# One core, a time-mix layer and then a routed block: statistics ahead of selection, another order on the scalar engine, and later gathers

## The chip, the cores and the metric

One core of a Trainium2 chip. The metric is device time in microseconds (us), from launch to end. A sequence's channels lie on the 128 partitions. The kernel is written for the engines directly, each with its own program and waits on semaphores: TensorE (PE), VectorE (DVE), ScalarE (ACT), GpSimd (POOL) and SyncE (SP, which issues loads and stores).

## What is computed

Two post-norm layers. The first, on 32 sequences of 512 tokens and 256 channels:

```python
x = layernorm(x + (sigmoid(r) * wkv(decay, first, k, v)) @ Wo)   # k, v, r from x mixed with its shift
# wkv: a = a*ew + exp(k)*v ; b = b*ew + exp(k), token by token
```

The second scores every token with a router (`x @ router_w`), takes per sequence the 63 best of 512, and runs a block on these alone:

```python
topv, topi = top_k(weights, 64); sel = sort(topi[:, :63])
x_sel, m_sel = x[sel], mask[sel][:, sel]
x1 = x_sel + softmax(rope(q) @ rope(k).T / 4 + m_sel) @ v @ wo   # 16 heads of 16
x2 = x1 + gelu(rmsnorm(x1) @ w1) @ w2
out = layernorm(x + scatter(x2 * weight) + x * (not selected))
```

## The kernel before

**First part (to 490 us).** A loop of 32 periods, one sequence each, written as four by hand, twelve in a loop over rings of four, and sixteen by hand. In period s the engines do:
- SP: `load_channels(s+2)`, `store_rows(s-3)`.
- POOL (`period`, L669): `differences_of(s+1)` (L561), `gate_of(s-1)` (L583), `mixes_of(s+1)` (three additions L567, one subtraction L568), `log_sum_of(s)` (L574), `scale_of(s-2)` (L590, L591). Every one is a tensor_tensor between buffers in SBUF but the copy L591.
- PE (L806): `projections(s)`, whose K, V and R parts each wait until DVE has done with the bank of sequence s-1 (`den_done`, `num_done`, `clamp_done`); `outputs(s-1)`; `selection(s)`.
- ACT (L1236): the exponentials, logarithms and reciprocals, `differences_scaled(s+1)` (L1185, L1186), `evacuation_of(s-1)` (L1193), `rows_of(s-3)` (L1215, the normalisation).
- DVE (L1561): `den_scan_of` (L1503), `den_of` (L1517), `products_of`, `clamp_of` (L1525), `num_of` (scans L1530, L1535), then `selection(s)`, then `statistics_of(s-1)` (L1544 to L1559).

The scans multiply by `ewb`, a [128, 2, 512] tile that the start fills with ones (L1455) and with the decay (L1483). Sequence 0 is mixed by DVE at the start (L1449, L1452); from sequence 1 on POOL and ACT mix.

**Selection.** The sequences fall into groups of 16, 12 and 4 (`SEQS`). For a group: `token_weights` (L1581 to L1587), PE turns them to rows, eight `top_round`s on DVE (a MAX8 L1624 and a MATCH_REPLACE8 L1626, the last without the replace), `slots_chosen` part 0 (L1635 to L1640) and part 1 (L1642 to L1644), PE turns the slots, `one_hot` (L1662) per pair, PE `picks`, `keep_values` (L1676 to L1686), which gives the row numbers for the gathers. Group 0's runs in periods 18 to 29; group 1's begins in period 29 and goes on in the attention.

**Attention (490 to 700 us).** Sixteen pairs of sequences. `att_period(n)` exists on each engine, and pairs overlap. PE's order (L1048) is: `mask_turn(n+1)` (L892), `project_qk(n)` (L917), `p_turn(n-2)` (L931), `project_v(n)`, `o_turn(n-3)` (L941), `scores(n-1)` (L967), `hn_turn(n+1)`, `mask_pick(n+1)` (L904), `values(n-2)`, `hn2_turn(n-4)`, `qk_turn(n)` (L975), `project_o(n-3)` with the group's turns and picks. ACT's order (L1351): `mask_copy`, `norm2_of(n-4)`, `pT_copy(n-2)`, `v_copy(n)`, in n = 1 the last sequences' variances, rows and roots, then `oT_copy`, `hnT_copy(n+1)` (L1233), `mask_keep`, `h2T_copy`, `exp_p(n-1)`, `q_copy`, `k_copy`. DVE's (L1855): `rope(n)`, `selection_early(n)`, `softmax_in(n-1)` (L1742 to L1746), `output_of`, `residual`, `selection_late(n)`. POOL's (L710): `normed2`, `rope_end`, gathers, `normed(n+2)`, `x_of(n+2)`, mask gathers. `x1`, the block's residual, lies from column 4096 of the arena, over the statistics' tiles.

**Last part (700 us to the end).** The feed-forward network over eight groups of two pairs, and the scatter. The change doesn't touch it.

## Time and profile before

| | us |
|---|---|
| median of 3 runs | 811.86 |
| lowest, highest | 810.51, 814.69 |
| the profiled execution | 812.5 |
| its span, first to last instruction | 810.8 |
| mean granted TensorE clock | 0.977 of 2.4 GHz |
| busy: PE, DVE, ACT, POOL | 92%, 83%, 65%, 61% |

A row of a timeline is: start, duration, engine, line, operation, output<-input, shape, count, and in brackets how long the engine was idle before it and what released it. "issue" as releaser means that no other engine's event shows. Rows of several instructions in a run are merged (x3), with the duration from the first's start to the last's end.

### The profile page before, as it was taken

Reading aid. Unit: us, or ns where it says so; the run is one execution under the profiler, and the core shown is the slowest. Engines: PE = TensorE matmul, PEld = TensorE weight load, DVE = VectorE, ACT = ScalarE, POOL = GpSimd, SP = SyncE. Lnnn points to the kernel's source line nnn. Section 1 sums busy time; section 2 is a strip of 40 time slices with the busy share of each in tenths; the row PEclk is TensorE's granted clock in tenths of the full one; section 3 lists DMA queues with packets and bytes.
Section 4 is the critical chain, followed back from the end, with each engine's and each line's share of the span. In section 5 each row is a group of like instructions: output and inputs, shape, how many; then the busy total and the mean of one; then the engine's idle time right before and its main releaser. Section 6 shows DMA issues by size and latency. Waiting matters only on the chain.

```text
span 810.8 us, 13316 instructions
## 1 busy us (share of the span) xinstructions
PE 743.9 (92%) x4482; PEld 551.1 (68%) x4482; DVE 675.3 (83%) x1382; ACT 523.7 (65%) x1015; POOL 498.5 (61%) x463
## 2 busy tenths in 40 slices
PE   7899999999999999899899986879998798899993
PEld 4566666666667666565557755667776577799993
DVE  7889989898989999999999999687798566257784
ACT  3668888888888887877666766646576566321120
POOL 1778878787878776787666995364556623202222
PEclk9999999999999999999999999899999899989998
DMA  8024232424232332332242112401110110000000
GB/s 227 2 65 118 80 116 65 129 65 125 69 107 88 96 100 66 101 94 65 68 120 73 46 50 88 143 27 47 39 36 14 50 43 2 1 1 28 27 20 34
DMA packets 37338, 55.41 MB, mean 68 GB/s; under 512 B 3360, under 2 KB 26528, under 8 KB 37280
## 3 DMA queue, kind: packets, MB, share of 16 engines
q1 hardware_dynamic: 34464, 46.28, 19.0%
q0 software_dynamic: 2816, 8.39, 3.4%
q8 instruction: 33, 0.54, 0.3%
q14 instruction: 25, 0.20, 0.1%
HBM read 35.78 MB, written 18.87 MB: 67 GB/s over the span
## 4 chain that ended last, share of the span: by engine, by line
PE 51%; DVE 24%; POOL 9%; issue 6%; ACT 6%; DMA 2%; SPq 0%; another core or an unknown queue 0%; POOLq 0%; DVEq 0%; ACTq 0%
PE ps L782 12%; PE ps L787 8%; PE ps L802 6%; PE ps L1112 5%; PE ps L1124 4%; POOL arena L567 4%; DVE arena L1503 3%; PE ps L917 2%; POOL arena L583 2%; PE ps L984 2%; DVE arena L1555 2%; PE ps L800 2%; DVE arena L1535 2%; DVE arena L1525 1%; DVE arena L1544 1%
## 5 line engine op out<-in xcount | busy, mean ns | idle before, releaser
L787 PE MATMUL ps<-halves 128*128 128x512 f32 x558 | 235.4, 530 | 0.0
L782 PE MATMUL ps<-arena,wa 128*128 128x512 f32 x384 | 201.9, 608 | 12.5 <-DVE arena L1535 4.4
L787 PEld LDWEIGHTS ps<-halves 128*128 128x128 f32 x558 | 106.0, 190 | 98.2 <-issue 89.9
L802 PE MATMUL ps<-wa,arena 128*128 128x256 f32 x512 | 133.0, 383 | 0.0
L583 POOL TENSOR_TENSOR arena<-arena 128x1024 f32<-128x1024 f32 x32 | 76.3, 2385 | 74.9 <-issue 53.1
L567 POOL TENSOR_TENSOR arena<-arena 128x512 f32<-128x512 f32 x93 | 116.8, 1288 | 5.3 <-ACT halves L1186 5.3
L782 PEld LDWEIGHTS ps<-arena,wa 128*128 128x128 f32 x384 | 69.8, 190 | 42.1 <-POOL halves L568 13.8
L802 PEld LDWEIGHTS ps<-wa,arena 128*128 128x128 f32 x512 | 88.2, 192 | 6.8
L1503 DVE TENSOR_TENSOR_SCAN arena<-ewb,ps 128x511 f32<-128x511 f32 x64 | 74.5, 1206 | 20.6 <-ACT ps L1158 19.2
L574 POOL TENSOR_TENSOR arena<-arena 128x1024 f32<-128x1024 f32 x32 | 76.4, 2387 | 23.6 <-ACT arena L1172 23.6
L1530 DVE TENSOR_TENSOR_SCAN arena<-ewb,ps 128x511 f32<-128x511 f32 x64 | 74.1, 1200 | 0.0
L1215 ACT ACTIVATE arena<-arena 128x256 f32<-128x256 f32 x128 | 66.1, 589 | 0.0
L638 POOL TENSOR_SCALAR arena<-arena,norm 128x256 f32<-128x256 f32 x16 | 16.6, 1036 | 74.5 <-ACT norm L1315 74.5
L1185 ACT ACTIVATE arena<-arena,cols 128x512 f32<-128x512 f32 x93 | 60.0, 710 | 0.0
L1344 ACT ACTIVATE arena<-ps 128x512 f32<-128x512 f32 x32 | 18.8, 598 | 61.6 <-PE ps L1112 61.6
L800 PE MATMUL ps<-ident,arena 128*128 128x128 f32 x256 | 49.5, 275 | 4.4 <-DVE arena L1555 2.8
L1112 PE MATMUL ps<-halves 128*128 128x256 f32 x384 | 50.4, 293 | 2.6 <-ACT arena L1336 2.6
L1112 PEld LDWEIGHTS ps<-halves 128*128 128x128 f32 x384 | 49.3, 202 | 3.2 <-ACT arena L1336 3.1
L1156 ACT ACTIVATE arena<-ps 128x1024 f32<-128x1024 f32 x32 | 32.6, 1020 | 26.2 <-PE ps L787 21.6
L800 PEld LDWEIGHTS ps<-ident,arena 128*128 128x128 f32 x256 | 35.9, 142 | 19.3 <-issue 3.8
L561 POOL TENSOR_TENSOR arena<-arena 128x512 f32<-128x512 f32 x31 | 41.5, 1339 | 12.1 <-DMA arena<-x_chan 12.0
L1124 PE MATMUL ps<-halves 128*128 128x256 f32 x384 | 47.5, 283 | 1.5 <-DVE halves L1893 1.5
(226 smaller groups left out, 1584.7 us busy)
## 6 DMA issues: line engine op xcount, KB each, us to landing
arena<-x_chan SPq DMA_DIRECT2D x32, 512.0 KB, 4.3
out<-arena SPq DMA_DIRECT2D x32, 512.0 KB, 3.3
arena<-x_chan SPq DMA_DIRECT2D x64, 127.8 KB, 3.4
wa<-w_attn SPq DMA_DIRECT2D x1, 1024.0 KB, 7.1
wa<-w_up SPq DMA_DIRECT2D x1, 1024.0 KB
wa<-w_down SPq DMA_DIRECT2D x1, 1024.0 KB
wqk<-w_qk SPq DMA_DIRECT2D x1, 512.0 KB, 5.2
wv<-w_v SPq DMA_DIRECT2D x1, 256.0 KB, 5.4
```

Of the source, the lines that this page charges most:

```text
L567: g.tensor_tensor(xm[s.par][:, m, :], xm[s.par][:, m, :], xs[s.k][:, :], ALU.add)
L574: g.tensor_tensor(ld[s.par][:, :, :], ld[s.par][:, :, :], er[s.par][:, :, :], ALU.add).then_inc(sum_done, 1)
L583: g.tensor_tensor(gg[s.par][:, :, :], num[s.par][:, :, :], ld[s.par][:, :, :], ALU.mult).then_inc(g_ready, 1)
L782: mm(bank[:, o, :], wa[:, m, 0, out_part], xm[s.par][:, m, :], start=True, stop=False)
L787: last = mm(bank[:, o, :], w[:, m, out_part], x[s.par], start=False, stop=(t == 2))
L800: mm(psY[:, j, c * P:(c + 1) * P], xc[s.k][:, c, tokens], ident[:, :], is_transpose=True, start=(c == 0), stop=False)
L802: last = mm(psY[:, j, :], gg[s.par][:, c, tokens], wa[:, 3, c, :], start=False, stop=(c == CC - 1))
L1112: last = mm(ps[:, k, h * GP * P:(h + 1) * GP * P], w[:, c, chunk], x[g.par][:, c, :], start=(c == 0 and t == 0), stop=(c == CC - 1 and t = ...
L1124: last = mm(ps[:, 4 + 2 * g.par + i, 0:C], x[:, f, i * P:(i + 1) * P], w[:, f, :], start=(f == 0 and t == 0), stop=(f == FC - 1 and t == 2))
L1215: last = a.activation(xt[s.k][:, j, :], xt[s.k][:, j, :], ACT.Identity, scale=stat[s.par][:, j, S2:S2 + 1], bias=nm[s.par][:, j:j + 1])
L1503: last = v.tensor_tensor_scan(bb[:, c, 1:T], ewb[:, c, 0:T - 1], psK[:, c, 0:T - 1], 0.0, ALU.mult, ALU.add)
L1530: v.tensor_tensor_scan(aa[:, c, 1:T], ewb[:, c, 0:T - 1], psV[:, c, 0:T - 1], 0.0, ALU.mult, ALU.add).then_inc(scan_a_done, 1)
```

## The change

It has these parts:
1. `ewb` goes; both scans take the decay column broadcast along the row. The tile's room stays as `shifted`, which holds only the attention's scores.
2. DVE mixes sequence 1 too at the start, after sequence 0 and the tables, and ACT rounds its second half in its own prologue. POOL does only the subtraction L568 for it.
3. In DVE's period the statistics come before the selection.
4. The last periods and the first pairs: `top_round(1, 1)` leaves period 31; PE does `project_qk(0)` ahead of `mask_turn(0)`; ACT does the last sequences' rows at the ends of pairs 1, 2 and 3, after q and k; POOL's last `scale_of` goes from pair 1 to pair 2. `x1` lies behind the statistics' tiles.
5. In every pair PE's `hn_turn` goes ahead of `scores`, and ACT's `norm2_of` behind `pT_copy` and `v_copy`.
6. Group 1's rounds and slots take one pair longer; group 2's begin one pair later and go two a pair. Gathers of pairs 8 to 10 move from pair 5 to pair 6, 11 to 13 from 7 to 8. For pairs 14 and 15 each mask gather is issued directly behind its row gather, ahead of `normed(14)`. `split_weight` moves from pairs 11 and 12 to 13 and 14.

```diff
@@ POOL
-                if nxt.exists():
+                if nxt.exists() and not is_start(at):
                     differences_of(nxt)
...
+                if not is_start(s.back(1)):
+                    for m in range(3):
+                        g.tensor_tensor(xm[s.par][:, m, :], xm[s.par][:, m, :], xs[s.k][:, :], ALU.add)
...
+                if q == 6:
+                    gather_rows(8, 4)
+                    gather_mask(8)
+                    gather_rows(9, 4)
+                    gather_rows(10, 4)
                 if q == 12:
                     for late in range(14, NP):
                         gather_rows(late, 6)
+                        gather_mask(late)
                 if q + 2 < NP:
                     normed(q + 2)
                     x_of(q + 2)
...
-                if q + 3 < 14:
+                if q + 3 < 14 and q != 5:
                     gather_mask(q + 3)
-                if q == 12:
-                    for late in range(14, NP):
-                        gather_mask(late)
@@ PE att_period
+                if n + 1 < NP:
+                    hn_turn(pair(n + 1))
                 scores(pair(n - 1))
                 if n + 1 < NP:
-                    hn_turn(pair(n + 1))
                     mask_pick(pair(n + 1))
@@ ACT att_period
-                if n == 2:
-                    rows_of(At(0, B - 1))
...
                 if n < NP:
                     v_copy(at)
-                if n == 1:
-                    variances_of(At(0, B - 1))
-                    rows_of(At(0, B - 3))
-                    logs_of(At(0, B - 1))
-                    rows_of(At(0, B - 2))
-                    roots_of(At(0, B - 1))
+                if 4 <= n < NP + 3:
+                    norm2_of(pair(n - 4))
...
                 if n < NP:
                     q_copy(at)
                     k_copy(at)
+                if n == 1:
+                    rows_of(At(0, B - 3))
+                    logs_of(At(0, B - 1))
+                    roots_of(At(0, B - 1))
+                if n in (2, 3):
+                    rows_of(At(0, B - 4 + n))
@@ DVE start
-            v.memset(ewb[:, :, :], 1.0).then_inc(ewb_made, 1)
...
+            dve.wait_ge(chan_in[1], 48)
+            dve.wait_ge(mixed, 1)
+            v.tensor_tensor(diff[:, :], xc[1][:, 0, :], xs[1][:, :], ALU.subtract).then_inc(diff_made, 1)
+            dve.wait_ge(diff_made, 2)
+            for m in range(3):
+                last = v.scalar_tensor_tensor(xm[1][:, m, :], diff[:, :], mix[:, m:m + 1], xs[1][:, :], ALU.mult, ALU.add)
+            last.then_inc(first_mixed, 1)
...
-                    last = v.tensor_tensor_scan(bb[:, c, 1:T], ewb[:, c, 0:T - 1], psK[:, c, 0:T - 1], 0.0, ALU.mult, ALU.add)
+                    last = v.tensor_tensor_scan(bb[:, c, 1:T], euw[:, 1, c:c + 1].to_broadcast([P, T - 1]), psK[:, c, 0:T - 1], 0.0, ALU.mult, ALU.add)
@@ DVE period
+                if at.had(1) and at.back(1).exists():
+                    statistics_of(at.back(1))
                 if isinstance(at.n, int):
                     selection(at.n)
-                if at.had(1) and at.back(1).exists():
-                    statistics_of(at.back(1))
...
-                if n == 31:
-                    top_round(1, 1)
```

DVE's selection per pair, before and after (r = a `top_round`, "early" is ahead of the softmax, "late" behind the residual):

| pair | before | after |
|---|---|---|
| 0 | r(1,2), r(1,3) | r(1,1), r(1,2) |
| 1 late | r(1,4), r(1,5), halves | r(1,3), r(1,4), halves |
| 2 late | r(1,6), r(1,7), `slots_chosen(1,0)`, `token_weights(2)` | r(1,5), r(1,6), r(1,7) |
| 3 | early: values 6, 7, `slots_chosen(1,1)` | early: values 6, 7; late: `slots_chosen(1,0)`, `token_weights(2)` |
| 4 | early: slots, `weights_copied(2)`, one_hot 8 to 10; late: r(2,0), halves | early: `slots_chosen(1,1)` |
| 5 | early: values 8 to 10; late: one_hot 11 to 13 | early: slots, `weights_copied(2)`, one_hot 8 to 10; late: r(2,0) |
| 6 | early: r(2,1); late: r(2,2) | early: values 8 to 10; late: one_hot 11, 12, r(2,1) |
| 7 | early: values 11 to 13; late: r(2,3), r(2,4) | early: one_hot 13; late: halves, r(2,2), r(2,3) |
| 8 | early: r(2,5); late: r(2,6) | early: values 11 to 13; late: r(2,4), r(2,5) |
| 9 | early: r(2,7); late: `slots_chosen(2,0)` | late: r(2,6), r(2,7), `slots_chosen(2,0)` |

From pair 10 on both are alike. PE's turns and picks move with them by one pair.

## Rows read from the trace of the kernel before

**Rows 1.** Engines' busy time by stretch: us, PE, PEld, DVE, ACT, POOL, granted clock, DMA.
```profile
26.00:264.00 238.00, 236.78 (x919) 158.28 (x920) 213.62 (x430) 195.51 (x324) 190.76 (x151) 1.00 0.29 87
264.00:490.00 226.00, 212.31 (x858) 142.74 (x859) 219.69 (x472) 169.39 (x295) 172.08 (x144) 0.98 0.26 80
490.00:690.00 200.00, 171.94 (x1793) 135.95 (x1792) 150.42 (x292) 124.20 (x337) 100.09 (x112) 0.97 0.16 49
```

**Rows 2.** Timeline of the start: DVE, then POOL, then PE.
```profile
8.92 2.08 DVE L1452 SCALAR_TENSOR_TENSOR arena<-arena,cols 128x512 f32<-128x512 f32 x3
...
14.55 1.93 DVE L1483 TENSOR_SCALAR ewb<-ewb,euw 128x512 f32<-128x512 f32 x2
...
24.99 1.23 DVE L1525 TENSOR_SCALAR arena<-ps 128x1024 f32<-128x1024 f32 x1 [1.03 <-ACT ps L1162]
...
14.93 1.27 POOL L561 TENSOR_TENSOR arena<-arena 128x512 f32<-128x512 f32 x1 [12.03 <-DMA arena<-x_chan]
...
25.15 1.28 POOL L568 TENSOR_TENSOR halves<-arena,halves 128x512 fp32r<-128x512 f32 x1
...
26.48 1.13 PE L782 MATMUL ps<-arena,wa 128*128 128x512 f32 x2 [2.56 <-POOL halves L568]
...
29.81 1.12 PE L782 MATMUL ps<-arena,wa 128*128 128x512 f32 x2
```

**Rows 3.** Timeline of DVE, selection in periods 18, 25, 26, 31 and in pair 2.
```profile
280.69 1.20 DVE L1584 TENSOR_SCALAR weights<-weights,rbb 128x64 f32<-128x64 f32 x1
...
374.97 2.33 DVE L1503 TENSOR_TENSOR_SCAN arena<-ewb,ps 128x511 f32<-128x511 f32 x2
...
388.24 2.74 DVE L1640 SCALAR_TENSOR_TENSOR wseq<-wseq,need 16x512 f32<-16x512 f32 x1
...
404.50 1.25 DVE L1643 TENSOR_TENSOR_SCAN wseq<-ones,wseq 16x512 f32<-16x512 f32 x1
405.78 1.59 DVE L1644 TENSOR_TENSOR wseq<-wseq 16x512 f32<-16x512 f32 x1
...
483.69 0.67 DVE L1624 MAX8 topv<-wseq 12x8 f32<-12x512 f32 x1
...
485.18 1.41 DVE L1544 BATCH_NORM_STATS2 arena<-arena 128x6 f32<-128x256 f32 x4
...
524.75 0.74 DVE L1640 SCALAR_TENSOR_TENSOR wseq<-wseq,need 12x512 f32<-12x512 f32 x1
```

**Rows 4.** Timeline of POOL beside the selection of periods 25 and 26.
```profile
388.06 2.37 POOL L583 TENSOR_TENSOR arena<-arena 128x1024 f32<-128x1024 f32 x1 [1.82 <-issue]
390.40 4.16 POOL L567 TENSOR_TENSOR arena<-arena 128x512 f32<-128x512 f32 x3
...
404.63 2.19 POOL L561 TENSOR_TENSOR arena<-arena 128x512 f32<-128x512 f32 x1
```

**Rows 5.** Timeline of PE in the attention.
```profile
488.87 1.16 PE L904 MATMUL ps<-halves,arena 128*128 128x128 f32 x8 [1.51 <-DVE arena L1733]
...
507.37 1.08 PE L975 MATMUL ps<-ident,arena 128*128 128x128 f32 x4 [4.82 <-ACT arena L1233]
...
509.10 3.62 PE L917 MATMUL ps<-wqk,arena 128*128 128x512 f32 x4
...
528.54 0.41 PE L941 MATMUL ps<-ident,arena 128*128 128x128 f32 x2 [3.23 <-DVE trig_part L1677]
...
537.04 1.88 PE L917 MATMUL ps<-wqk,arena 128*128 128x512 f32 x4
...
618.83 1.88 PE L917 MATMUL ps<-wqk,arena 128*128 128x512 f32 x4
...
645.09 1.12 PE L892 MATMUL ps<-ident,arena 128*128 128x128 f32 x4 [4.00 <-DMA arena<-mask_rows,msk_i]
```

**Rows 6.** Timeline of ACT in pair 1, second group of rows.
```profile
504.41 2.06 ACT L1215 ACTIVATE arena<-arena 128x256 f32<-128x256 f32 x4
```

**Rows 7.** Timeline of POOL, the first late mask gather of pair 12.
```profile
641.77 1.01 POOL L609 DMA_INDIRECT arena<-mask_rows,msk_i  x1 [0.16 <-issue]
```

More of the change, by code:

```diff
@@ L208, in rwkv_then_selected_block_kernel @@
         h2T = place(CC, NP * P)
+        top[0] = after_stats
         x1 = place(NP, C)
+        assert top[0] <= MIXED
         top[0] = MIXED
@@ L440, in tables_of, with is_start @@
             return 2 if 2 * first + 1 < MB else 1
+        def is_start(at):
+            return isinstance(at.n, int) and at.n == 0
         def pair(n):
@@ L560, in differences_of @@
                 pool.wait_ge(scaled, s.n)
+                if is_start(s.back(2)):
+                    pool.wait_ge(first_mixed, 1)
                 g.tensor_tensor(diff[:, :], xc[s.k][:, 0, :], xs[s.k][:, :], ALU.subtract).then_inc(diff_made, 1)
@@ L771, in projections @@
                 pe.wait_ge(mixed, s.n + 1)
-                if isinstance(s.n, int) and s.n == 1:
+                if is_start(s.back(1)):
                     pe.wait_ge(w1_split, 1)
+                    pe.wait_ge(first_mixed, 1)
                 for m, bank, ready, used in ((0, psK, k_ready, den_done), (1, psV, v_ready, num_done), (2, psR, r_ready, clamp_done)):
@@ L1090, in _ @@
             hn_turn(pair(0))
+            project_qk(pair(0))
             mask_turn(pair(0))
-            project_qk(pair(0))
             project_v(pair(0))
@@ L1150, in _ @@
             a.activation(w1_hi, wa[:, 0:3, 1, :], ACT.Copy).then_inc(w1_rounded, 1)
+            act.wait_ge(chan_in[1], 48)
+            a.activation(x1_hi[1], xc[1][:, 1, :], ACT.Copy).then_inc(scaled, 1)
             def exp_k_of(s):
@@ L1240, in period @@
                     reciprocal_of(at.back(1))
-                if at.back(-1).exists():
+                if at.back(-1).exists() and not is_start(at):
                     differences_scaled(at.back(-1))
```

87 lines of the change are left out of this document (41 added, 46 removed).

## The prediction

> **What bounds the kernel now.** I read the busy time by stretch first, then each engine's timeline where the bound changes. Three stretches differ [rows 1]. From 26 to 264 us PE is busy 236.78 of 238 us at full clock: whatever another engine saves there is worth nothing, and whatever delays PE once at the start is kept to the end. From 264 to 490 us DVE is busy 219.69 of 226 us, more than PE's 212.31: the selection has been laid on a DVE that was nearly full, so each microsecond more on DVE counts in full. From 490 to 690 us no engine is full: PE works 171.94 of 200 us, DVE 150.42. The time there goes in chains between engines, and 28 us of PE's idling is the most that a better order can win. The last stretch, where PE is the bound, isn't touched.
>
> **Part by part.** About 0.5% of the time, 4 us, is what a measurement of this kernel can tell from no change.
>
> *Start.* The tile of decays costs DVE 1.93 us for its scaling [rows 2] plus its fill. Both go; the scans keep their length, as the scan over broadcast ones does (1.25 us for 512 elements [rows 3], the same as over a full tile). In their place DVE mixes sequence 1: a difference, for which I take 0.7 us as for one of the three mixing instructions, and those three at 2.08 [rows 2]. It can't start before the channels land at 14.93. PE now idles 2.56 us for POOL's mixing of sequence 1 before 26.48, and that goes. But it is given back at once: the V part of the same sequence starts at 29.81 and needs `num_done` of sequence 0. That chain hangs on DVE's clamp at 24.99, which itself waited 1.03 us for ACT, and so for PE's projection of sequence 0, which the change leaves alone. So the gain is 0. The cost: while DVE mixes, POOL has its one subtraction L568 ready, 1.28 us [rows 2], and the two engines exclude each other (below). The mixing, the router column and the split of the weights then end about 2 us later than before; 1 us of it is swallowed by the 1.03 us wait, and +1.0 is left, kept in full through the PE-bound stretch. Bounds 0 and +1.5; I take +1.0, since both become ready in the same microsecond.
>
> *Statistics ahead of selection.* DVE's work is the same sum in another order. What changes is what POOL does beside it. An instruction with two SBUF inputs is held until POOL's present tensor_tensor ends: L1640 took 2.74 us in period 25 beside POOL's gate (388.06 to 390.43) and 0.74 undisturbed [rows 3, 4]; L1584, one input and a column, took 1.20 beside L561. It goes both ways, by turns: POOL's next three additions took 4.16 instead of 3 times 1.24, and L561 took 2.19 beside the scan L1643, after which L1644 took 1.59. The rounds (MAX8 and replace, 1.49 from 483.69 to 485.18) keep their time and don't matter here.
> The gate starts 13.1 us after the period's first scan (388.06 less 374.97) and is followed by four instructions of 1.24 us: POOL is dense for 7.3 us. The selection used to start 9.6 us into the period, at the end of a log sum and over one difference. The statistics take 3.2 us, so it now starts at 12.8 us, just where the train begins. Period 18 gains 1.6 (before the gate there is room for its seven small instructions, and L1584 and its neighbour aren't held). Period 20: L1597 waits out the gate, +1.4. Period 25: copy, two comparisons, scan and L1640, five instructions that each wait for one of POOL's five, so that they end with the train at 23 us instead of 19.2: +3.7. Period 26: L1642 to L1644 wait for the rest of the gate and two additions, +2.6. Periods 27 and 28: -1.9, as the one-hots fall into a gap and the wait for PE's picks (0.75) is covered by the statistics. Period 29: +1.0. Sum +5.2. Lower end: if the comparisons of period 25 aren't held and period 26 finds a gap, 0. Upper end, every heavy period ends with the train: +9.
> The Trainium skill's page "SBUF — State Buffer", section "SBUF: two separate sides", makes the pair of ports that DVE and GpSimd share "an exclusive lock, not a bandwidth split", taken by fast-mode instructions with a single input as well, and says that GpSimd's own DMAs can't write their descriptors while DVE holds it. By that, all five of period 25 are held, as in my sum; with two-input instructions alone it would be 2 of 5 and +1.5. What it adds is the third rival.
>
> *Last period and pair 0.* The round taken from period 31 lets the statistics, the mask's copy and then PE's `mask_pick(0)` (488.87, idle 1.51 for it) come 1.4 earlier: -1.4. The reordering of `mask_turn(0)` and `project_qk(0)` hides under the same wait, 0. The round is done in pair 0, beside `outputs(31)`.
>
> *ACT's order.* At 507.37 PE had idled 4.82 us for `hnT_copy(2)` on ACT [rows 5], which stood behind two groups of rows of 2.06 [rows 6] and small ones. Now `hnT_copy` comes right after `v_copy`, and the next to be late is the softmax of pair 0 (DVE), for the mask turn of pair 3. Scores end 0.7 after `project_v(1)` and one `hn_turn`, the softmax's three instructions take 3.7, and PE has 1.6 of picks and turns to do meanwhile: 2.1 of idling stay. So -2.7. The long idling was followed by half clock: `project_qk(2)` took 3.62 instead of 1.88 [rows 5], and the turns around it about twice theirs. That goes: -2.6. Each of the three groups of rows now delays `mask_copy` and `pT_copy` by 2.1, hidden while PE still does its projections.
> *Pair 2's selection.* At 528.54 PE had idled 3.23 us for values 6 and 7: DVE had done two rounds, `slots_chosen(1,0)` and `token_weights(2)` before, and `slots_chosen(1,1)` then held up the softmax. Three rounds (3.7) stand there now; the wait falls to 0.7, and the mask turn of pair 5 no longer waits for a softmax behind slots. -3.5. Together `project_qk(4)` starts at 537.04 - 10.2.
> *Pairs 4 to 10.* What was put off has to be done: in pairs 6 to 10 DVE has 54 us (rope 1.4, softmax, output and residual 4.6 to 5, the rest from the table), PE 52. Before, DVE had 48. I followed the chain pair by pair: in pair 6 the mask of pair 8 is 0.7 late, in pair 8 `keep_values(11 to 13)` holds `o_turn` 2.3 us, in pair 10 the slots hold the softmax 1.6 longer. `project_qk(11)` comes at 618.83 - 7.6: +2.6 given back.
> *Pair 12.* PE idles 4.00 us for the mask of pair 14 at 645.09. The gather was issued at 641.77 and PE went on 3.3 later [rows 5, 7]. Placed behind the row gather, ahead of the second one, `normed` and `x_of`, it goes out 3.6 earlier; PE is free at 641.1, so 0.4 to 1.3 of idling stay: -3.1. Half clock followed here too; with it -5.1. `split_weight`'s later place delays the load of the down weights by two pairs, with 5 us in hand before their use.
> *`norm2_of` later.* `pT_copy` comes 1 us earlier and `normed2` 2 us later, ahead of `rope_end` on POOL; PE's small wait for the one becomes a small wait for the other. 0, bounds -3 and +3.
>
> Attention: -1.4 -2.7 -2.6 -3.5 +2.6 -5.1 = -12.7. **Sum:** +1.0 +5.2 -12.7 = -6.5. The profiled execution took 812.5 us, 0.6 above the median of the runs, so from the median: 811.86 - 6.5 = **805.4**.
>
> **Rivals.**
> 1. *The train doesn't bite.* POOL's gate follows PE and ACT, not DVE; if it shifts by a microsecond, the selection falls between. Then the first part costs 0 to +1: 800 to 801. For it: period 21 to 24's rounds can't be held. Against: the 13.1 is the same in every DVE-bound period I looked at. 0.18.
> 2. *DVE becomes the attention's bound.* Its 54 us in pairs 6 to 10 chain through softmax and picks, and each pair waits: another +3 to +5 is given back, and the sum is -2.5: about 809.4. For it: four waits that I found lie on DVE. Against: PE has nearly as much work. 0.18.
> 3. *Gathers late.* With four issues in a row in pair 6, a mask row lands after PE wants it, in pairs 6 and 8, 2 us each, and long idling brings the half clock back (2 us): 811. By the page above each issue could also wait for a one-hot (0.6). 0.08.
> 4. *Slower: DVE and POOL hold each other.* Place: periods 25 to 29. The held selection also holds POOL's additions, which are on PE's chain to the next K. If each instruction of `keep_values`, `token_weights` and the one-hots waits for one of POOL's, five periods grow by 4 to 5 us each, +22, and -12.7 leaves +9: 821. It decides from +13 in the first part upwards. 0.08.
> 5. *The scan over a broadcast column is slower.* At +3% of 128 scans of 1.2 us it is only 4.6 on DVE, half of it hidden: 808. 0.03.
>
> My forecast keeps 0.45. **Range** 798.5 to 812.5: from rival 1 with the attention's -14 to rival 3 with one more microsecond; it leaves out rival 4 and the tails. **Chances:** faster by over 0.5% (below 807.8): 0.36 of the 0.45, all of rival 1, and 0.1 of the others, 0.64. Within 0.5%: 0.28. Slower: 0.08.
>
> **What would show it.** Start: PE's V part of sequence 1 at about 30.8 instead of 29.81. First part: period 25 of about 23 us, L1640 and its neighbours long; the first attention projection of pair 0 some 4 to 6 us later than before. Attention: no wait of over 3 us on PE, no L917 run over 2 us; PE's idling from pair 0 to the last pair down by 8 or more. If the first part keeps its length, my reading of the turns on the ports is wrong; if pairs 6 to 10 take over 60 us, the DVE rival is right.

## The result and the profile after

The changed kernel took 816.79 us (median of 20 executions, 812.60 to 824.79) against 812.59 us for the kernel before (20 executions, 809.96 to 818.54): ratio 1.0057, 95% interval 1.0035 to 1.0078. Measured again on another chip the ratio was 1.0052 (1.0020 to 1.0083). It is slower. 805.4 us was forecast with a range of 798.5 to 812.5, and 0.08 on slower. The profiled execution took 814.5 us, span 812.5; it is a good one among the 20, so what it shows explains about 2 of the 4 us. Ratios leave out executions more than 1.5% above the fastest of their kernel.

| stretch, from and to | before | after | after, 2nd profile | forecast |
|---|---|---|---|---|
| first scans of sequences 2 to 31 | 428.3 | 432.2 | 428.6 | +5.2 |
| `project_qk` of pairs 0 to 4 | 52.7 | 45.3 | 44.2 | -8.8 |
| pairs 4 to 11 | 81.8 | 91.5 | 95.4 | +2.6 |
| pairs 11 to 15 | 48.3 | 47.1 | 47.2 | -5.1 |
| pair 15 to the end | 143.7 | 141.1 | 142.6 | 0 |

Each stretch is the difference of two starts in a timeline. Between the first two rows, from the first scan of sequence 31 to `project_qk(0)`, the kernel after is 0.7 us shorter (9.5 for 10.3). The last row has no part of the change in it that was given a price, and it lies between 140.7 and 144.2 us over all twenty profiles of this case, so its -2.6 is no gain of the change.

The same three stretches as in [rows 1] of the kernel after, and pairs 6 to 10 (the columns are those of rows 1):

```profile
26.00:264.00 238.00, 234.80 (x914) 157.04 (x912) 213.53 (x429) 195.64 (x324) 190.28 (x150) 1.00 0.29 87
264.00:490.00 226.00, 212.48 (x844) 143.86 (x845) 216.85 (x453) 167.16 (x284) 169.03 (x143) 0.96 0.27 79
490.00:690.00 200.00, 174.02 (x1776) 135.47 (x1774) 149.13 (x306) 123.41 (x340) 98.66 (x112) 0.97 0.17 50
559.00:625.00 66.00, 56.76 (x567) 43.75 (x566) 51.42 (x103) 36.76 (x104) 34.42 (x37) 0.95 0.13 37
```

The kernel before in pairs 6 to 10:

```profile
561.00:619.00 58.00, 52.72 (x566) 41.75 (x565) 49.26 (x88) 38.19 (x108) 32.66 (x35) 1.00 0.13 38
```

In 264 to 490 us the granted clock fell from 0.98 to 0.96; in pairs 6 to 10 it fell from 1.00 to 0.95, and PE idled 9.2 us instead of 5.3 (66 less 56.76, 58 less 52.72). So of the 8 us that these pairs are longer, 3.9 are waits and 4.0 are PE working longer on the same matmuls, at the lower clock. DVE is busy for 78% of these pairs: it isn't full, but it is late at two places.

Timeline of DVE after: the first scans of sequences 0 and 2, then the selection of period 25, the place of [rows 3]:

```profile
20.26 2.32 DVE L1521 TENSOR_TENSOR_SCAN arena<-euw,ps 128x511 f32<-128x511 f32 x2
...
45.82 2.33 DVE L1521 TENSOR_TENSOR_SCAN arena<-euw,ps 128x511 f32<-128x511 f32 x2 [0.65 <-ACT ps L1173]
...
370.83 2.33 DVE L1521 TENSOR_TENSOR_SCAN arena<-euw,ps 128x511 f32<-128x511 f32 x2
...
384.04 2.31 DVE L1653 COPY thr_rows<-topv 16x64 f32<-16x64 f32 x1
386.27 1.54 DVE L1654 TENSOR_SCALAR wseq<-wsrc,topv 16x512 f32<-16x512 f32 x1
387.75 1.25 DVE L1655 TENSOR_SCALAR ties<-topv 16x63 f32<-16x63 f32 x1
389.03 2.22 DVE L1656 TENSOR_TENSOR_SCAN wseq<-ones,wseq 16x512 f32<-16x512 f32 x1
391.18 0.18 DVE L1657 TENSOR_REDUCE need<-ties 16x1 f32<-16x63 f32 x1
391.39 1.46 DVE L1658 SCALAR_TENSOR_TENSOR wseq<-wseq,need 16x512 f32<-16x512 f32 x1
392.89 2.33 DVE L1521 TENSOR_TENSOR_SCAN arena<-euw,ps 128x511 f32<-128x511 f32 x2
```

and of POOL beside it, as in [rows 4]:

```profile
383.92 2.38 POOL L593 TENSOR_TENSOR arena<-arena 128x1024 f32<-128x1024 f32 x1 [1.83 <-issue]
386.26 3.91 POOL L577 TENSOR_TENSOR arena<-arena 128x512 f32<-128x512 f32 x3
390.14 2.17 POOL L578 TENSOR_TENSOR halves<-arena,halves 128x512 fp32r<-128x512 f32 x1
```

The five instructions are held as forecast: the copy ends with POOL's gate at 386.3, the comparisons, the scan and L1658 end one after another beside POOL's four instructions, which run to 392.3, and period 25 lasts 22.06 us (370.83 to 392.89) instead of 19.21. A comparison of 63 elements (L1655) takes 1.25 us and a copy of 64 (L1653) 2.31; in pair 10, where POOL is idle, the same two lines take 0.23 and 0.18 us, on 4 partitions instead of 16.

PE after, the attention, as in [rows 5]:

```profile
508.73 0.63 PE L904 MATMUL ps<-ident,arena 128*128 128x128 f32 x4 [2.15 <-DVE shifted L1762]
509.19 1.88 PE L929 MATMUL ps<-wqk,arena 128*128 128x512 f32 x4
...
521.45 3.29 PE L929 MATMUL ps<-wqk,arena 128*128 128x512 f32 x4
...
532.78 1.88 PE L929 MATMUL ps<-wqk,arena 128*128 128x512 f32 x4
...
573.72 0.66 PE L904 MATMUL ps<-ident,arena 128*128 128x128 f32 x4 [3.16 <-DMA arena<-mask_rows,msk_i]
...
616.76 1.13 PE L916 MATMUL ps<-halves,arena 128*128 128x128 f32 x8 [1.92 <-DVE arena L1779]
...
623.77 0.41 PE L904 MATMUL ps<-ident,arena 128*128 128x128 f32 x2 [1.69 <-DVE shifted L1762]
624.23 1.88 PE L929 MATMUL ps<-wqk,arena 128*128 128x512 f32 x4
...
649.31 0.66 PE L904 MATMUL ps<-ident,arena 128*128 128x128 f32 x4 [3.24 <-DMA arena<-mask_rows,msk_i]
649.80 2.86 PE L929 MATMUL ps<-wqk,arena 128*128 128x512 f32 x4
```

Pair 1's wait is 2.15 us instead of 4.82, pair 4 begins at 532.78 instead of 537.04. But in pair 6 there is a new wait of 3.16 us for a mask row, and in pair 12 the old one has only shrunk from 4.00 to 3.24. The queue of POOL says why (pair 6, then pair 12, as in [rows 7]):

```profile
566.61 0.93 POOL L648 TENSOR_SCALAR arena<-arena,norm 128x256 f32<-128x256 f32 x1 [10.73 <-ACT norm L1330]
567.50 1.40 POOL L640 TENSOR_TENSOR arena<-arena 128x256 f32<-128x256 f32 x2
569.05 1.03 POOL L612 DMA_INDIRECT arena<-out,row_i  x1 [0.15 <-issue]
570.39 0.95 POOL L619 DMA_INDIRECT arena<-mask_rows,msk_i  x1 [0.31 <-issue]
...
642.20 0.92 POOL L648 TENSOR_SCALAR arena<-arena,norm 128x256 f32<-128x256 f32 x1 [7.74 <-ACT norm L1330]
643.09 1.40 POOL L640 TENSOR_TENSOR arena<-arena 128x256 f32<-128x256 f32 x2
644.64 1.03 POOL L612 DMA_INDIRECT arena<-out,row_i  x1 [0.15 <-issue]
645.97 0.95 POOL L619 DMA_INDIRECT arena<-mask_rows,msk_i  x1 [0.30 <-issue]
```

`normed2` (L648) is first in POOL's queue in each pair, and it waits for ACT's `norm2_of`, which the change put behind `pT_copy` and `v_copy`. The mask gather stands behind it, behind the two additions of `rope_end` and a row gather. In pair 12 it goes out at 645.97, 4.2 us later than the 641.77 of [rows 7], but by then the whole pair stands 4.8 us later: counted from `project_qk(12)`, which begins at 631.36 before and at 636.18 after, the gather goes out 9.8 us into the pair instead of 10.4. So the place that the change moved forward in the table brought 0.6 us, where 3.6 were forecast. PE goes on 3.3 us after it, as before.

### The profile page after: what moved, and what is told of

It is laid out like the page before. It is cut to its first block, busy times and chain, and to the rows that moved or that the text cites. A ratio compares the mean times of both kernels' runs of the same rounds, so it can differ in the third digit from the quotient of the medians.

```text
span 812.5 us, 13308 instructions
## 1 busy us (share of the span) xinstructions
PE 747.4 (92%) x4482; PEld 552.9 (68%) x4482; DVE 673.9 (83%) x1383; ACT 522.5 (64%) x1012; POOL 490.9 (60%) x459
## 4 chain that ended last, share of the span: by engine, by line
PE 37%; DVE 20%; POOL 19%; issue 18%; ACT 3%; DMA 1%; SPq 1%; POOLq 0%; DVEq 0%; ACTq 0%
PE ps L794 11%; PE ps L799 8%; PE ps L814 6%; PE ps L1125 5%; PE ps L1137 4%; DVE arena L1521 3%; POOL arena L640 3%; POOL arena L577 3%; POOL arena L593 2%; DVE arena L1543 2%; POOL arena L627 2%; DVE arena L1548 2%; DVE arena L1573 2%; DVE arena L1562 2%; DVE ps L1528 2%
## 5 line engine op out<-in xcount | busy, mean ns | idle before, releaser
L794 PE MATMUL ps<-arena,wa 128*128 128x512 f32 x384 | 204.3, 614 | 14.7 <-DVE arena L1535 5.9
L577 POOL TENSOR_TENSOR arena<-arena 128x512 f32<-128x512 f32 x90 | 114.3, 1302 | 0.1
L794 PEld LDWEIGHTS ps<-arena,wa 128*128 128x128 f32 x384 | 71.1, 193 | 43.1 <-POOL halves L578 10.4
L1521 DVE TENSOR_TENSOR_SCAN arena<-euw,ps 128x511 f32<-128x511 f32 x64 | 74.4, 1204 | 20.5 <-ACT ps L1173 20.2
L1548 DVE TENSOR_TENSOR_SCAN arena<-euw,ps 128x511 f32<-128x511 f32 x64 | 74.1, 1200 | 0.0
L648 POOL TENSOR_SCALAR arena<-arena,norm 128x256 f32<-128x256 f32 x16 | 15.8, 990 | 93.7 <-ACT norm L1330 93.7
L1200 ACT ACTIVATE arena<-arena,cols 128x512 f32<-128x512 f32 x90 | 58.0, 708 | 0.1
L812 PE MATMUL ps<-ident,arena 128*128 128x128 f32 x256 | 48.9, 273 | 1.8 <-POOL arena L593 1.8
L1125 PE MATMUL ps<-halves 128*128 128x256 f32 x384 | 47.9, 284 | 2.6 <-ACT arena L1351 2.6
L1177 ACT ACTIVATE ps<-ps 128x1024 f32<-128x1024 f32 x32 | 32.3, 1008 | 26.7 <-PE ps L799 21.8
L1137 PE MATMUL ps<-halves 128*128 128x256 f32 x384 | 47.5, 283 | 1.5 <-DVE halves L1910 1.5
L578 POOL TENSOR_TENSOR halves<-arena,halves 128x512 fp32r<-128x512 f32 x31 | 41.2, 1330 | 12.4 <-ACT halves L1165 12.4
```

The lines of the kernel that those rows point to most:

```text
L577: g.tensor_tensor(xm[s.par][:, m, :], xm[s.par][:, m, :], xs[s.k][:, :], ALU.add)
L794: mm(bank[:, o, :], wa[:, m, 0, out_part], xm[s.par][:, m, :], start=True, stop=False)
L1125: last = mm(ps[:, k, h * GP * P:(h + 1) * GP * P], w[:, c, chunk], x[g.par][:, c, :], start=(c == 0 and t == 0), stop=(c == CC - 1 and t = ...
L1137: last = mm(ps[:, 4 + 2 * g.par + i, 0:C], x[:, f, i * P:(i + 1) * P], w[:, f, :], start=(f == 0 and t == 0), stop=(f == FC - 1 and t == 2))
L1200: a.activation(xm[s.par][:, m, :], diff[:, :], ACT.Copy, scale=mix[:, m:m + 1])
L1521: last = v.tensor_tensor_scan(bb[:, c, 1:T], euw[:, 1, c:c + 1].to_broadcast([P, T - 1]), psK[:, c, 0:T - 1], 0.0, ALU.mult, ALU.add)
```

## The experiments

Theories at the outset: A, the first part's +3.9 us is DVE held by POOL (statistics ahead of the selection); B, it is half clock of PE, a matter of chance; C, the attention's loss is the late `norm2_of` ahead of the gathers in POOL's queue; D, it is DVE's added load in pairs 6 to 10 (rival 2 of the prediction). Ratios are to the kernel before on the same chip, with 95% intervals, from 12 executions of each kernel (10 in one) and 15 to 35 of the kernel before. Chips differ: the kernel before had medians of 812.2 to 820.0 us on them, so only ratios are compared.

**One part of the change undone, on one chip.**

*Selection ahead of statistics again.*
```diff
+                if isinstance(at.n, int):
+                    selection(at.n)
                 if at.had(1) and at.back(1).exists():
                     statistics_of(at.back(1))
-                if isinstance(at.n, int):
-                    selection(at.n)
```


> The changed kernel with one part undone: in a period of the first part the selection stands ahead of the statistics again. Theory A (DVE's slots, weights and picked values are held by POOL's gate and its four instructions when they begin 3 us later in the period): sequence 31's first scan comes at about 474 us instead of 477.97, period 25 lasts 19.2 and not 22.1 us, and the time is 3.8 us under the changed kernel's: ratio to the kernel before 1.001. Rival B (the first part is longer through half clock of PE in periods 27 and 28, whatever DVE's order): the start of sequence 31 moves by 2 us or less, ratio 1.003 to 1.006.


Ratio 0.9984 (0.9949 to 1.0019). Period 25 lasts 19.22 us, and sequence 31 begins 428.2 us after sequence 2. The loss of the change goes away with it. But the first part shows little of that: unchanged, it takes 428.6 us in one of its two profiles, so this order is worth 0.4 us there, and the rest of the gain isn't in it.

*The kernel before with statistics first alone.*


> The kernel before with one part of the change alone: statistics ahead of the selection in each period of the first part. Theory A (the turns on the shared ports between DVE and POOL): sequence 31's first scan at 478 to 479 us instead of 474.14, period 25 at 22 us, the time 4 us over the kernel before, ratio 1.005. If the first attention pair waits less for the mask copy, up to 1 us of that is won back. Rival B (half clock, a matter of chance): ratio 1.000 to 1.002 with period 25 under 20.5 us.


Ratio 1.0043 (1.0006 to 1.0081), period 25 22.06 us, sequence 31 430.9 us after sequence 2, so +2.6. The rest is clock: the mean granted clock of its 12 executions was 0.960 against 0.967. So A and B may go together: the new order costs little by itself and may cost more through the clock.

*`norm2_of` ahead of `pT_copy` again.*
```diff
+                if 4 <= n:
+                    norm2_of(pair(n - 4))
...
                 if 2 <= n < NP + 2:
                     pT_copy(pair(n - 2))
                 if n < NP:
                     v_copy(at)
-                if 4 <= n < NP + 3:
-                    norm2_of(pair(n - 4))
```


> The changed kernel with norm2_of back ahead of pT_copy on ACT. Theory C (in pairs 6 and 12 POOL's normed2 waits for ACT's later norm2_of, up to 10 us in pair 6, and rope_end and the gathers of the mask rows stand behind it; PE then idles 3.2 us for a mask row in pairs 8 and 14 and runs at half clock after): both idlings fall under 1 us, PE's second rotary turn no longer waits for POOL, and the time is 4 to 6 us under the changed kernel's, ratio 0.998 to 1.001. Rival D (DVE is the attention's bound in pairs 6 to 10, and its load did not change): the masks come earlier but PE then waits for the softmax or the picked values; pairs 6 to 11 still take 62 us or more, gain 2 us or less, ratio 1.004 or more.


Ratio 0.9952 (0.9925 to 0.9979): this kernel is faster than the one before. Its POOL in pairs 6 and 12, and its PE for the same mask rows:

```profile
557.82 0.92 POOL L648 TENSOR_SCALAR arena<-arena,norm 128x256 f32<-128x256 f32 x1 [8.72 <-ACT norm L1330]
...
563.22 0.95 POOL L619 DMA_INDIRECT arena<-mask_rows,msk_i  x1 [0.30 <-issue]
...
636.68 0.92 POOL L648 TENSOR_SCALAR arena<-arena,norm 128x256 f32<-128x256 f32 x1 [4.98 <-ACT norm L1330]
...
642.13 0.95 POOL L619 DMA_INDIRECT arena<-mask_rows,msk_i  x1 [0.30 <-issue]
```

```profile
566.61 0.66 PE L904 MATMUL ps<-ident,arena 128*128 128x128 f32 x4 [0.41 <-DMA arena<-mask_rows,msk_i]
...
645.52 0.66 PE L904 MATMUL ps<-ident,arena 128*128 128x128 f32 x4 [0.48 <-DMA arena<-mask_rows,msk_i]
```

Both waits are gone (0.41 and 0.48 us), as theory C has it, and pairs 11 to 15 take 43.2 us instead of 47.1. In pair 12 the gather goes out 6.8 us after `project_qk(12)` (642.13 less 635.30), 3.6 earlier than in the kernel before, as forecast. Pairs 6 to 11 still take 67.0 us: that stretch is long for another reason than the late `norm2_of`.

*The tables of the kernel before* (rounds, slots, picks, gathers, `split_weight` in their old pairs; all else changed).


> The changed kernel with the tables of the second and third group's selection as in the kernel before: rounds, slots, picks, gathers and the split of the weights in their old pairs. Theory C: norm2_of is still late on ACT, so normed2 still holds rope_end and the gathers; POOL-bound waits of PE stay, pair 2's wait of 3 us for values 6 and 7 is back, and the time is within 2 us of the changed kernel's, ratio 1.003 to 1.008. Rival D (the rounds moved into pairs 6 to 9 are what makes DVE late there): pairs 6 to 11 take 57 to 59 us instead of 65, pairs 2 to 5 lose 3.5, and the time is 3 to 4 us under the changed kernel's, ratio 1.001 to 1.002.


Ratio 1.0016 (0.9985 to 1.0048). Pairs 6 to 11 take 55.1 us, even less than rival D said, while pairs 0 to 6 take 80.6 instead of 71.9, and pair 12 waits 6.92 us for the mask of pair 14: with the gather in its old place and `norm2_of` late it is worse than in either kernel.

**The changed kernel again, and three variants, on a second chip.**

*The changed kernel as it is.*


> The changed kernel as it is, beside three variants of it, to see how much of its first part and of its idlings is the same in every execution. If the kernel's loss is in its order of work: ratio 1.004 to 1.008, period 25 22.06 us and period 26 18.08 again, PE idling about 3.2 us for a mask row in pairs 6 and 12 again. If the loss of 3.1 us in period 28 (20.05 us here, 16.77 in the kernel with norm2_of back, with the same first part) is half clock by chance, period 28 lies at 16.8 to 18.5 us now. If the loss was a matter of the chip or the day: ratio under 1.002.


Ratio 1.0052 (1.0020 to 1.0083); the medians of all executions, 819.39 us and 818.34, lie closer together than that. Periods 25 and 26 took 22.06 and 18.10 us, the two waits for mask rows 3.28 and 3.28 us: these belong to the order of work. Period 28 took 16.76 us instead of 20.05: that one was chance.

*`norm2_of` early and the selection first.*


> The changed kernel with norm2_of ahead of pT_copy and the selection ahead of the statistics, both as in the kernel before. If the two losses are separate and add: what is left of the change is ACT's rows, pair 2's selection and the gathers, ratio 0.990 to 0.993 (6 to 8 us faster than before). If the first part's loss was mostly half clock by chance, this kernel is no faster than the one with norm2_of alone: ratio 0.994 to 0.997.


Ratio 0.9944 (0.9900 to 0.9988). Only 8 of its 12 executions are counted; the medians of all are 815.08 us and 818.34. Both undone is no sum of the two gains; the interval doesn't tell it from `norm2_of` alone, so once `norm2_of` is early, the order in the first part makes no difference that can be told.

*The same with the selection first in periods 25, 26 and 29 only.*
```diff
+                early = isinstance(at.n, int) and at.n in (25, 26, 29)
```


> As the last one, but with the selection ahead of the statistics in periods 25, 26 and 29 alone, where the two orders differ by 2.85, 1.8 and 1.6 us against the new one, and the new order in 18 to 24, 27, 28 and 30, where it wins 1.9, 0.2, 1.2, four times 0.2, 1.3, 0.2 and 0.2. Theory A (the turns on the ports hold the selection only where it falls beside POOL's gate and the four instructions after it): period 25 19.2 us, period 26 16.3, and sequence 31 begins 5 to 6 us earlier after sequence 2 than in the kernel before (428.29 us), ratio 0.984 to 0.988. Rival (the shift of the statistics only carries the same work from one period into the next, so that the gains go with the losses): 428 us or more after sequence 2, ratio as that of the kernel before last within 0.002.


Ratio 0.9994 (0.9962 to 1.0025), a miss. Sequence 28 begins 375.0 us after sequence 2, against 380.5 in the kernel before: the 5.5 us are there. But period 28 took 20.05 us and period 29 17.31 at a low clock, and sequence 31 came 427.0 after sequence 2; in pairs 6 to 11 the clock was low as well. The gain ahead of the picks was lost behind them.

*Late `norm2_of`, but `rope_end` and the gathers ahead of `normed2` on POOL.*


> The changed kernel with normed2 behind rope_end and the gathers on POOL, norm2_of late on ACT as changed. Theory C in its narrow form (it is the place of the gathers behind a waiting normed2 on POOL's queue that costs, not ACT's order by itself): PE's idling for the mask rows of pairs 8 and 14 falls from 3.2 us to under 1 and its waits for rope_end go; hn2_turn may wait up to 1 us for normed2. Ratio 0.996 to 1.001, as with norm2_of early. Rival (ACT's order itself costs, by a later residual copy and exp): ratio 1.004 or more.


Ratio 0.9985 (0.9951 to 1.0019), better than the changed kernel beside it, but PE waits as long as before, now for `normed2` itself:

```profile
573.73 0.69 PE L1014 MATMUL ps<-ident,arena 128*128 128x128 f32 x2 [3.19 <-POOL arena L648]
...
652.82 0.69 PE L1014 MATMUL ps<-ident,arena 128*128 128x128 f32 x2 [3.26 <-POOL arena L648]
```

So it isn't only the queue's order: if the gathers don't wait for `norm2_of`, `normed2` itself is what PE waits for. What made this kernel faster than the changed one isn't shown: its one profile has pairs 6 to 11 at 66.6 us and 11 to 15 at 47.4, as there.

**On a third chip.**

*`norm2_of` early, selection first, old tables: the start and ACT's rows are left of the change.*


> The changed kernel with three parts undone: norm2_of ahead of pT_copy, selection ahead of statistics, and the tables of the second and third group as in the kernel before. What is left of the change is its start, ACT's rows and hn_turn's place. If the tables are the source of what the change wins (pair 2's selection, the earlier gathers): ratio 0.999 to 1.001, worse than 0.9944 with the new tables, and pair 12 of PE has an idling of over 3 us for a mask row again. If ACT's rows win by themselves (pair 1 shorter by 3.1 us, from 11.3 to 8.2): ratio 0.994 to 0.997. If the new tables cost in pairs 6 to 10 as much as they win before: the same 0.994 as with them.


Ratio 1.0017 (0.9984 to 1.0049). Pair 1 lasts 8.16 us, 3.1 less, and pair 3 17.54 instead of 15.35.

*The kernel before with `norm2_of` later alone.*


> The kernel before with one part of the change alone: norm2_of behind v_copy on ACT. Theory C (normed2 waits longer for it on POOL, with rope_end and the gathers behind): POOL's normed2 waits 1.5 to 2 us longer in each pair, PE idles for rope_end in the rotary turn, and the idling of 4.00 us for the mask of pair 14 grows to 5 us or more; ratio 1.003 to 1.006. Rival (the late norm2_of costs only together with the gathers' new place a pair later): ratio 0.998 to 1.002.


Ratio 1.0069 (1.0043 to 1.0095), the dearest part of all by itself. The wait for the mask of pair 14 grew from 4.00 [rows 5] to:

```profile
654.75 1.11 PE L892 MATMUL ps<-ident,arena 128*128 128x128 f32 x4 [6.83 <-DMA arena<-mask_rows,msk_i]
655.66 3.55 PE L917 MATMUL ps<-wqk,arena 128*128 128x512 f32 x4
```

with half clock after it, and the gather behind L638, which had waited:

```profile
644.05 0.92 POOL L638 TENSOR_SCALAR arena<-arena,norm 128x256 f32<-128x256 f32 x1 [6.96 <-ACT norm L1315]
...
651.40 1.01 POOL L609 DMA_INDIRECT arena<-mask_rows,msk_i  x1 [0.15 <-issue]
```

*`norm2_of` early, statistics first, and PE kept busy.*
```diff
-                for j in range(TJ):
+                for j in list(warm) + list(range(TJ)):
...
+                    outputs(at.back(1), {26: range(TJ), 27: range(3)}.get(at.n, ()) if isinstance(at.n, int) else ())
```


> The changed kernel with norm2_of back ahead of pT_copy, and in periods 26 and 27 PE computes the output projection of the sequence before twice over (the same values; in period 27 three of its four token blocks), so that it is busy where it otherwise idles 5.5 us and 3.7 us in one piece. Theory E (what statistics ahead of selection costs is PE's long idling for DVE, after which it runs at half clock for microseconds, in periods 26 to 28): the granted clock from 390 to 450 us rises from 0.92 on average to 0.97 or more, period 28 stays at 16.8 us, and the ratio is 2 to 3 us better than with norm2_of alone: 0.991 to 0.994. Rival (the half clock there has nothing to do with the idling, or the added matmuls only delay PE's own work): ratio 0.995 to 0.999.


Ratio 0.9969 (0.9937 to 1.0000). The windows from 390 to 460 us, first of the kernel with `norm2_of` early, then of this one:

```profile
390.00:460.00 70.00, 60.33 (x257) 41.77 (x257) 67.89 (x147) 45.06 (x74) 44.54 (x36) 0.93 0.24 70
```

```profile
390.00:460.00 70.00, 66.42 (x305) 48.12 (x304) 68.46 (x144) 43.48 (x71) 45.67 (x36) 0.98 0.23 70
```

PE's idling before K of sequence 27 fell from 5.53 to 1.22 us, the clock rose from 0.93 to 0.98, and period 28 took 16.22 us instead of 16.76: theory E's mechanism. That it gains time isn't shown; the ratio is no better than without it.

*`norm2_of` early, selection first, and the third group's slots behind the softmax.*
```diff
-                if n == 9:
                     top_round(2, 6)
+                if n == 9:
                     top_round(2, 7)
...
-                if n == 10:
-                    slots_chosen(2, 1)
...
                     output_of(pair(n - 2))
+                if n == 10:
+                    slots_chosen(2, 1)
```


> The changed kernel with norm2_of early and selection first (0.9944), and on DVE the third group's seventh round in pair 8 instead of 9, and slots_chosen(2, 1) behind the softmax and the output of pair 10 instead of ahead. Theory F (in pairs 9 and 10 DVE is what PE waits for: 2.1 us for the rotary part and 1.7 us for the softmax): pair 10 lasts 11.5 to 12.5 us instead of 14.4, both waits under 1 us, ratio 0.990 to 0.992. Rival (the wait only moves to the third group's copy of slots in pair 11, or to pair 8): ratio 0.994 to 0.996.


Ratio 0.9961 (0.9932 to 0.9989), no better than without it (0.9944), as the rival had it: pair 10 took 15.6 us, and PE waited for the slots instead:

```profile
623.38 0.54 PE L843 MATMUL ps<-ident,wseq 4*128 4x4 f32 x4 [3.14 <-DVE wseq L1661]
```

**On a fourth chip: what was still open.**

*The start alone.*


> The kernel before with the change's start alone (the scans over a broadcast column, DVE mixing sequence 1, no subtraction on POOL for it). If the start costs what was forecast, 1.0 us: sequence 2's first scan 1 us later, ratio 1.001 to 1.002. If it is hidden, as the trace of the changed kernel has it (45.82 against 45.85 us): ratio 0.999 to 1.001, and all of the 1.0017 of the start with ACT's rows is ACT's. If it shifts the clock's low stretch at the start: sequence 2's first scan between 44.9 and 48.9 us from run to run, as in the kernels so far.


Ratio 1.0010 (0.9986 to 1.0035), no difference that can be told. Sequence 2 began at 48.75 us here, at 44.9 to 48.9 in the kernels with the start and at 45.2 to 48.9 in those without.

*ACT's rows alone (with `hn_turn` and `mask_turn(0)`).*


> The kernel before with ACT's rows behind hnT_copy, PE's hn_turn ahead of the scores and mask_turn(0) behind project_qk(0) alone. Forecast: ratio 0.993 to 0.995 (5.3 us). If the gain of pair 1 (11.28 to 8.16 us) is given back in pair 3, where PE waits for the picked values 6 and 7 on DVE and was late anyway: pair 3 lasts 17 to 18 us instead of 15.35, project_qk(4) comes less than 1 us earlier, ratio 0.998 to 1.002.


Ratio 0.9995 (0.9968 to 1.0022). `project_qk(4)` began 2.7 us nearer to pair 0 than before, but pair 4 lasted 16.32 us instead of 13.65, and pairs 0 to 6 took 76.8 instead of 77.1.

*Mixed order, slots behind the softmax, two blocks twice in period 27.*


> The kernel with the mixed order (selection first in 25, 26 and 29 alone) and norm2_of early, with the third group's slots behind the softmax in pair 10, its seventh round in pair 8, and two token blocks of the output projection computed twice in period 27, where PE waits 1.9 us for the clamp. If the half clock in period 28 (20.05 us) was a matter of that idling: period 28 at 16.3 to 17 us, sequence 31 begins 422 to 424 us after sequence 2, ratio 0.986 to 0.990. If it comes from the picks' short matmuls (16 and 32 columns) ahead of period 28 and not from the idling: period 28 at 18 to 20 us again, ratio 0.993 to 0.997, no better than the kernel beside it.


Ratio 0.9954 (0.9922 to 0.9986), no better than the next. Period 28 took 18.83 us at a low clock, so the idling before the picks isn't all of its cause.

*`norm2_of` early, selection first, once more.*


> The changed kernel with norm2_of early and selection first once more, beside the last one: ratio 0.993 to 0.997 if the first measurement (0.9944) holds.


Ratio 0.9960 (0.9932 to 0.9987), median 807.92 us against 812.17. Twice measured, it beats the kernel before and with it the changed one. Its pairs 6 to 10, with the columns of rows 1:

```profile
557.00:619.00 62.00, 57.52 (x568) 45.34 (x567) 53.02 (x103) 35.87 (x103) 35.69 (x37) 0.92 0.13 37
```

PE idles 4.5 us here (62 less 57.52), less than the 5.3 of the kernel before, and works 4.8 us longer, at a clock of 0.92 instead of 1.00. So with `norm2_of` early these pairs are still longer than before, by low clock and not by waits.

**The tables alone, on two more chips.**

> The kernel before with the tables of the second and third group's selection, the gathers' and split_weight's places of the changed kernel alone, the start, ACT's order and the first part as they were. If the tables win while norm2_of is early: ratio 0.992 to 0.996, pair 3 about 12 us instead of 15.35, no idling of over 1.5 us for a mask row in pair 12, pairs 6 to 10 longer by 4 to 7 us. If DVE's added load in pairs 6 to 10 gives all of it back: ratio 0.998 to 1.002. The five parts alone would then sum to +0.6% (first case) or +1.1% (second case) beside the +0.55% measured for all together.


Ratio 1.0047 (1.0022 to 1.0071), but not a clean run of the part: the tables put POOL's `scale_of` for the last sequence a pair later, and ACT's rows, in their old place ahead of `pT_copy`, wait for it:

```profile
518.83 2.07 ACT L1216 ACTIVATE arena<-arena 128x256 f32<-128x256 f32 x4 [7.08 <-POOL arena L590]
```

> The tables alone as in the last run, with POOL's scale_of for the last sequence in its old place, in pair 1. If the 7 us of pair 2 were that wait and nothing else: pair 2 at 12 to 13 us, ratio 0.995 to 0.999 (some of the wait was in parallel with one of 4.8 us earlier and of what DVE needs for rounds). If the tables cost by themselves: ratio 1.002 or more.


Ratio 1.0011 (0.9987 to 1.0035): pair 2 back at 11.07 us, pair 3 10.55 instead of 15.35, pairs 11 to 15 43.7 instead of 48.3, and pairs 6 to 11 67.5 instead of 57.3, at a clock of 0.90. What the tables win, they give back. The run before, with the same tables, had a clock of 1.00 in those pairs, and they took 59.2 us (it had lost 7 us in pair 2, in which DVE could work ahead): much of the 10 us is clock, then.

## Why the prediction was wrong

**`norm2_of` later: 0, bounds -3 and +3.** This is the step that turned the sign. "A small wait for the one becomes a small wait for the other" looked at `normed2` and `rope_end` only; the gathers stand in the same queue behind both, and by them hang the mask rows, for which PE waits in full. Alone it cost 0.69%, over 5 us; taken back from the changed kernel it turned 1.0052 to 1.0057 into 0.9952 (on another chip). The prediction named `rope_end` as queued behind `normed2` and did not go further down the queue to the DMAs. Rival 3 had a mask row late, but for four issues in a row; with the same issues and `norm2_of` early the wait is 0.41 us. Rival 4, which held the chance of slower, had periods 25 to 29 growing by 4 to 5 us each, and none did for its reason: 2.85, 1.8, -1.3, -0.2 and 1.6 where the clock stayed up.

With this step taken back, 0.9952 is 3.9 us faster, within the range, but in part by luck. In that profile the start and the first part, forecast at +6.2, gave -0.8 (sequence 2 at 44.88 us, sequence 31 428.5 us behind it), and pairs 4 to 11, forecast at +2.6, gave +14.1 (95.9 us): two errors of opposite sign, the second the larger.

**Pair 12: -5.1.** The gather was to go out 3.6 us earlier in the pair and went out 0.6 earlier, for the same cause. Pairs 11 to 15 gained 1.1 to 1.2 us. With `norm2_of` early they gained 5.1: the term was right, and its condition gone.

**Pairs 4 to 10 give back +2.6.** By size this term was the furthest off: they gave back 9.7 and 13.6 us (pairs 4 to 11). The mask of pair 8 was to be 0.7 us late and was 3.16. The sign of rival 2, pairs 6 to 10 over 60 us, came (64.9 and 67.7), but its mechanism, each pair waiting for DVE, is only a part of it: DVE was busy 51.4 us and not 54, and of the 8 us, 3.9 were waits, the late mask among them, and 4.0 low clock, which the term didn't have at all. The length stays with `norm2_of` early (61.1 to 67.2 in the seven profiles of variants of the changed kernel) and goes with the old tables (54.7 to 58.2 in the six other kernels that have them, 57.3 in the kernel before). The waits on DVE are for the rotary part and the softmax of pair 10 (1.92 and 1.69 us), behind two rounds and the slots. DVE, at 78%, isn't the bound. Why the new tables go with a lower clock in these pairs isn't shown.

**First part: +5.2, and +1.0 at the start.** The mechanism of period 25 was right in each of its five instructions: +2.85 for +3.7 forecast. The Trainium skill's page "SBUF — State Buffer", section "SBUF: two separate sides", has fast-mode instructions with a single input held too, and the trace agrees as far as it shows (not the mode): the copy took 2.31 us and the two comparisons 1.54 and 1.25. Period 26 gave +1.8 for +2.6, 29 +1.6 for +1.0. But period 20, forecast at +1.4, gave -1.2; 18 gave -1.9 for -1.6, and 19 and 21 to 24 -0.2 each for 0; 27 and 28 gave -1.5 for -1.9 where the clock stayed up. In sum the reordering costs 0.4 us, not 5.2, where the clock is as before: the fastest first part with it took 428.5 us, and without it 428.1. What it cost beyond that is half clock. In six profiles with the new order and PE not kept busy the first part took 428.5 to 432.2 us, 430.3 on average; in eleven with the old one 429.1, eight of them 428.1 to 428.3; with the new order and PE kept busy it took 428.2. Three of the eleven took 431.0 to 431.6, by half clock from period 28 on as well, so the 1.2 us between the averages aren't shown to be the order's. The start's +1.0 isn't there (45.82 for 45.85). The V part of sequence 1 began at 29.88 us, as in the kernel before (29.81 [rows 2]), not at 30.8.

**ACT's order and pair 2: -1.4, -2.7, -2.6, -3.5.** Right up to pair 4: 45.3 us for 52.7, -7.4, and -8.4 in the second profile, for -8.8 with the last period left out (there 0.7 us came for 1.4). The remaining wait of 2.1 us came out at 2.15. The -2.6 for the clock did not hold: it was half again at 521.45 (3.29 us), a pair later. And the gain doesn't last by itself: ACT's rows alone measured 0.9995. Of the signs named for the attention none came: PE waited over 3 us twice (3.16, 3.24), L929 (the L917 of before) ran over 2 us four times, and PE's idling from 490 to 690 us fell by 2 us (28.1 to 26.0), not by 8.

**The parts don't add.** Alone they cost +0.10 (start), -0.05 (ACT), +0.43 (statistics), +0.69 (`norm2_of`) and +0.11% (tables), in sum +1.3%, against +0.55% together. Each has an interval of 0.25 to 0.4% to either side, so that the sum is uncertain by some 0.6% (an estimate, the five errors taken as independent), and the difference is only just clear of it. From the changed kernel, taking back `norm2_of` gave about 1.0%, statistics 0.7%, the tables 0.4%, each measured on another chip than the changed kernel itself. `norm2_of` loses either way. The statistics lose alone and in the changed kernel, and make no difference that can be told once `norm2_of` is early (0.9952 with them first, 0.9944 and 0.9960 without). Of the tables and ACT's order each seems to pay only with the other (alone 1.0011 and 0.9995): both with `norm2_of` early and the selection first gave 0.9944 and 0.9960.

**Open.** Why the statistics alone cost 0.43% when the first part shows 0.4 to 2.6 us of it. By numbers it is clock: that kernel's mean of 0.960 against 0.967 is 4.9 us at the 0.7 us for each thousandth found below, more than all of the loss. One piece of it comes with the order: in each of the six profiles with the new order and PE not kept busy PE idles 5.5 us ahead of K of sequence 27 and the granted clock from 390 to 410 us is 0.83, and in each of the eleven with the old one its longest wait in that window is 2.8 us and the clock 0.91. But PE has room there, and the rest lies elsewhere: the one profile of that kernel has its pairs 0 to 6 at 84.3 us, at a clock of 0.83 from 490 to 560 us, and nothing in the order of those pairs differs from the kernel before.

## What to carry to other kernels

Where an edit delays one instruction, go down the queue of every engine that waits for it to the last DMA issue, and ask when its data is wanted; here the place of one call in ACT's table decided the sign of the whole change. A pair made shorter by idle time is a gain only if the pairs behind it aren't late by themselves, so sum an order of work to the next place where the engines meet, not to the first wait removed. And test a forecast's "0, small wait for small wait" first: it is where nothing was worked out.

## What the runs showed of the hardware

The clock is a term of its own. On one chip executions of the kernel before went from 812.98 us at a mean granted clock of 0.978 to 824.39 at 0.962, some 0.7 us for each thousandth. So two kernels whose orders differ by 1 us can measure 4 apart, and one profile of each can't rank them: the changed kernel's period 28 took 20.05 us in one profile and 16.76 in another, with the same code. Half clock came with long idling of PE (the 4.82, 6.83 and 5.5 us waits), but also where no wait in the 50 us before it had been longer than 2.8 us: in the kernel with `norm2_of` early and the selection first it came in the middle of the picks ahead of period 28 (matmuls of 16 and 32 columns), and the same picks ran at full clock in the kernel before.

Small DVE instructions pay the whole hold: a copy of 64 elements on 16 partitions took 2.31 us beside POOL's gate and a comparison of 63 took 1.25 beside its additions (0.18 and 0.23 on 4 partitions with POOL idle), so the count of held instructions matters and not their size.
